# x1 in the output tensor, accumulating DMAs from GpSimd, the last bias on VectorE, and one more high half on ScalarE in each second quad

## What is computed

```
x1  = x + xattn(layernorm(x), ctx, ctx) @ wo          # 16 heads; correlation, top 4 lags, softmax, mix
h   = gelu(q16(layernorm(x1)) @ q8(W_in) + b_in)      # 256 -> 1024
out = x1 + q16(h) @ q8(W_out) + b_out                 # 1024 -> 256
```

## Time and profile before

| | |
|---|---|
| median of 3 runs | 1096.88 us (1096.68 to 1096.90) |
| the profiled execution | 1096.63 us, its span 1094.8 us |
| TensorE clock granted over the span | 0.988 |
| busy: PE, DVE, ACT, POOL | 97%, 89%, 86%, 46% of the span |
| moved by DMA | 203 GB/s over the span, 327 to 356 GB/s in most slices of part 3 |

### The profile page before, as it was taken

The page is one execution under the profiler, slowest core; times in us unless marked ns, Lnnn a source line. Parts: engine busy times, 40 slices in busy tenths (PEclk is TensorE's granted clock), DMA queues, the critical chain, the costliest instruction groups (busy, mean ns, idle before and its releaser), DMA issues.

```text
span 1094.8 us, 28979 instructions
## 1 busy us (share of the span) xinstructions
PE 1057.6 (97%) x9303; PEld 773.7 (71%) x9303; DVE 973.0 (89%) x2790; ACT 944.1 (86%) x1698; POOL 505.2 (46%) x674
## 2 busy tenths in 40 slices
PE   6999999999999999999997799999997999999998
PEld 4788778888888888887786344444443888888886
DVE  2799998888888888888888799999997999999998
ACT  4788989988888888888886588888888999999996
POOL 4888888888888888888885400000000000000000
PEclk9999999999999999999998899999998999999999
DMA  5533334433333333333330299999999899999995
GB/s 174 169 118 116 117 110 130 131 118 117 116 118 117 117 117 117 118 117 121 122 118 37 90 310 305 307 307 307 307 307 356 313 344 334 348 327 343 347 347 200
DMA packets 141426, 222.59 MB, mean 203 GB/s; under 512 B 72321, under 2 KB 92161, under 8 KB 137217
## 3 DMA queue, kind: packets, MB, share of 16 engines
q1 hardware_dynamic: 140224, 220.12, 59.4%
q10 hardware_dynamic: 1088, 1.05, 0.3%
HBM read 121.00 MB, written 83.89 MB: 187 GB/s over the span
## 4 chain that ended last, share of the span: by engine, by line
PE 61%; DVE 11%; issue 9%; ACT 2%; DMA 1%; DVEq 1%; POOL 1%; ACTq 0%; SPq 0%; POOLq 0%
PE bank L559 20%; DVE arena L1244 7%; PE bank L420 6%; PE bank L469 6%; PE bank L493 6%; PE bank L433 6%; PE bank L443 4%; PE bank L481 4%; PE bank L455 4%; PE bank L508 3%; DVE arena L1237 2%; DVE arena L1259 1%; PE bank L588 1%; ACT arena L813 1%; DMA arena<-x_scratch 1%
## 5 line engine op out<-in xcount | busy, mean ns | idle before, releaser
L588 PE MATMUL bank<-wout,arena 128*128 128x256 f16 x2048 | 236.1, 274 | 4.4 <-DVE arena L1237 3.0
L588 PEld LDWEIGHTS bank<-wout,arena 128*128 128x128 f16 x2048 | 196.4, 98 | 45.7 <-DVE arena L1244 12.2
L559 PE MATMUL bank<-arena,win 128*128 128x512 f16 x1024 | 222.5, 381 | 2.6 <-DVE arena L1195 2.6
L559 PEld LDWEIGHTS bank<-arena,win 128*128 128x128 f16 x1024 | 100.4, 98 | 124.5 <-issue 4.1
L1244 DVE SCALAR_TENSOR_TENSOR arena<-arena,wout_rel 128x512 f16<-128x512 int16 x256 | 183.1, 746 | 3.9 <-ACT arena L813 1.3
L770 ACT ACTIVATE arena<-bank,b_in_sb,z_scale 128x512 f32<-128x512 f32 x192 | 147.0, 777 | 15.2 <-PE bank L559 10.1
L608 ACT ACTIVATE arena<-bank 128x512 f32<-128x512 f32 (+1 forms) x196 | 116.0, 593 | 31.6 <-PE bank L420 25.8
L608 ACT ACTIVATE arena<-arena 128x512 f16<-128x512 f32 x192 | 114.3, 624 | 2.4 <-POOL arena L873 0.7
L806 ACT ACTIVATE arena<-arena,one 128x1536 int16<-128x1536 f32 x64 | 100.2, 1567 | 18.5 <-DVE arena L1244 15.4
L1209 DVE TENSOR_REDUCE hmax<-arena 128x1 f32<-128x1024 f32 x96 | 111.2, 1210 | 2.9 <-ACT arena L770 2.9
L813 ACT ACTIVATE arena<-arena,wout_rel 128x512 f16<-128x512 int16 x160 | 106.9, 706 | 0.0
(11 more groups left out here) (121 smaller groups left out, 2061.6 us busy)
## 6 DMA issues: line engine op xcount, KB each, us to landing
hidden_scratch<-arena SPq DMA_DIRECT2D x32, 1536.0 KB, 5.6
arena<-hidden_scratch SPq DMA_DIRECT2D x64, 768.0 KB, 7.1
arena<-in_ctx_turned SPq DMA_DIRECT2D x64, 256.0 KB, 3.0
arena<-in_x_turned SPq DMA_DIRECT2D x64, 256.0 KB, 3.5
arena<-in_x SPq DMA_DIRECT2D x64, 256.0 KB, 3.2
x_scratch<-arena SPq DMA_DIRECT2D x64, 256.0 KB, 2.0
arena<-x_scratch SPq DMA_DIRECT2D x32, 512.0 KB, 6.0
out<-arena SPq DMA_DIRECT2D x32, 512.0 KB, 4.1
```

The lines of the kernel that those rows point to most:

```text
L559: last = nc.tensor.matmul(bank[f][:, :].rearrange("p (n t) -> p n t", n=4), win16[:, f, c, :], xt[q % 3][:, s, :, c, :], start=s == 0 and ...
L588: last = nc.tensor.matmul(bank[m * 2 + k // 2][:, k % 2 * D:(k % 2 + 1) * D], gbuf[:, s, f, k * P:(k + 1) * P], wout16[:, f, :], start=f = ...
```

## The change

`x1_scratch` goes. Part 1 stores its x1 rows straight into the output tensor. In part 3 `finish` computes scale times PSUM plus b_out (read from SBUF with a broadcast over the batches) into `yq[m]`, and GpSimd adds `yq[m]` to the rows in the output with an accumulating DMA. For the last quad it is otherwise: its x1 rows are loaded back into SBUF (`last_rows`), GpSimd adds b_out to them, VectorE adds the scaled PSUM in `finish_last`, and SyncE stores them. TensorE's bias matmuls go with GpSimd's chains and the semaphores between them. `finish` now waits for the accumulating DMA of the quad before last in place of the x1 load. In quads of odd number ScalarE makes the high half of chunk 4 as well, between high 3 and `to_int` of the next quad, and VectorE doesn't.

```diff
-HIGH_ON_ACT = (1, 3, 5, 6, 7)
+HIGH_ON_ACT = ((1, 3, 5, 6, 7), (1, 3, 4, 5, 6, 7))
+HIGHS = sum(len(v) for v in HIGH_ON_ACT)
...
-        bias_f = store_x[:, 0:256]
-        bias_rest = store_x[:, 256:512]
-        bias_part = store_x[:, 512:640].bitcast(BF16)
-        bias_rows = store_x[:, 640:768].bitcast(BF16)
-        bias_cut = store_x[:, 768:896].bitcast(BF16)
-        y_rows = store_x[:, 896:960].bitcast(BF16)
-        y_part = store_x[:, 960:962].bitcast(BF16)
-        y_rest = store_x[:, 964:967]
-        y_col = store_x[:, 968:971]
+        last_rows = store_x[:, 0:1024]
...
-        act_high = lambda q, f: q * len(HIGH_ON_ACT) + (HIGH_ON_ACT.index(f) + 1)
-        dve_high = lambda q, f: q * (FC - len(HIGH_ON_ACT)) + (f + 1 - sum(g < f for g in HIGH_ON_ACT))
+        def act_high(pairs, m, f):
+
+            return pairs * HIGHS + (m * len(HIGH_ON_ACT[0]) + HIGH_ON_ACT[m].index(f) + 1)
+
+        def dve_high(pairs, m, f):
+
+            return pairs * (2 * FC - HIGHS) + (m * (FC - len(HIGH_ON_ACT[0])) + f + 1 - sum(g < f for g in HIGH_ON_ACT[m]))
...
-                sp.dma_start(x1_v[p], x1.rearrange("p b d -> p (b d)")).then_inc(s_x1_st, 16)
+                sp.dma_start(out_q[p // 2, :, p % 2 * 2 * D:(p % 2 + 1) * 2 * D], x1.rearrange("p b d -> p (b d)")).then_inc(s_x1_st, 16)
...
-            def load_x1(q, m):
-                wait(sp, s_out[m], 16 * ((q - m) // 2) if isinstance(q, int) else (q - m) * 8)
-                sp.dma_start(yq[m].rearrange("p (n k) -> p n k", n=2), rows(x1_q, q)).then_inc(s_x1_ld[m], 16)
-
-            def store(q, m):
-                wait(sp, S["c_out"], (q + 1) * 2)
-                sp.dma_start(rows(out_q, q), yq[m]).then_inc(s_out[m], 16)
...
-            sp.wait_ge(S["b_max"], QUADS * FC // 2)
-            load_x1(0, 0)
-            load_x1(1, 1)
-            def load_quad(q, m):
-                for part in range(2):
-                    load_hidden(q, m, part)
-
-            load_quad(2, 0)
-            load_quad(3, 1)
-            store(0, 0)
-            with sp.Fori(1, QUADS // 2 - 1) as i:
+            sp.dma_start(last_rows, out_q[QUADS - 1]).then_inc(s_last, 16)
+            with sp.Fori(0, QUADS // 2 - 1) as i:
                 for m in range(2):
-                    load_quad(i * 2 + (m + 2), m)
-                    load_x1(i * 2 + m, m)
-                    store(i * 2 + (m - 1), 1 - m)
-            load_x1(QUADS - 2, 0)
-            store(QUADS - 3, 1)
-            load_x1(QUADS - 1, 1)
-            store(QUADS - 2, 0)
-            store(QUADS - 1, 1)
-            for m in range(2):
-                sp.wait_ge(s_out[m], 16 * (QUADS // 2))
+                    for part in range(2):
+                        load_hidden(i * 2 + (m + 2), m, part)
+            sp.wait_ge(S["c_out"], QUADS * 2)
+            sp.dma_start(out_q[QUADS - 1], last_rows).then_inc(s_last, 16)
+            sp.wait_ge(s_last, 32)
+            sp.wait_ge(s_out[0], 16 * (QUADS // 2))
+            sp.wait_ge(s_out[1], 16 * (QUADS // 2 - 1))
...
-            def output(q, m):
+            def output(q, m, pairs):
                 wait(pe, S["c_out"], (q - 1) * 2)
                 for f in range(FC):
-                    if f in HIGH_ON_ACT:
-                        wait(pe, S["c_hi_act"], act_high(q, f))
+                    if f in HIGH_ON_ACT[m]:
+                        wait(pe, S["c_hi_act"], act_high(pairs, m, f))
                     else:
-                        wait(pe, S["c_hi_dve"], dve_high(q, f))
+                        wait(pe, S["c_hi_dve"], dve_high(pairs, m, f))
                     for s in range(2):
                         if s == 1:
                             wait(pe, S["c_lo"], q * FC + (f + 1))
                         for k in range(4):
                             last = nc.tensor.matmul(bank[m * 2 + k // 2][:, k % 2 * D:(k % 2 + 1) * D], gbuf[:, s, f, k * P:(k + 1) * P],
                                                     wout16[:, f, :], start=f == 0 and s == 0 and k % 2 == 0,
-                                                    stop=False, skip_group_check=True)
-                    if f == FC - 1:
-                        pe.wait_ge(S["bias_ready"], 1)
-                        for j in range(2):
-                            last = nc.tensor.matmul(bank[m * 2 + j][:, :].rearrange("p (b d) -> p b d", b=2), y_rows, bias_rows.unsqueeze(1).broadcast_to([P, 2, D]),
-                                                    start=False, stop=True, skip_group_check=True)
+                                                    stop=f == FC - 1 and s == 1, skip_group_check=True)
                     last.then_inc(S["c_f"], 1)
...
                 high(q, 3)
+                if 4 in HIGH_ON_ACT[m]:
+                    high(q, 4)
                 if more:
                     to_int(q + 1, 1 - m, 0)
                 high(q, 5)
...
-            pool.wait_ge(S["xm_ready"], 1)
             pool.wait_ge(S["b_out_in"], 16)
...
-            then(nc.gpsimd.tensor_copy(bias_part, b_out_sb[:, :]))
...
-            pool.wait_ge(S["y_inverse"], 1)
...
-            nc.gpsimd.tensor_scalar(y_rows, y_rows, y_col[:, 0:1], None, ALU.mult).then_inc(S["bias_ready"], 1)
+            pool.wait_ge(s_last, 16)
+            nc.gpsimd.tensor_tensor(last_rows.rearrange("p (b d) -> p b d", b=4), last_rows.rearrange("p (b d) -> p b d", b=4),
+                                    b_out_sb[:, :].unsqueeze(1).broadcast_to([P, 4, D]), ALU.add).then_inc(S["bias_added"], 1)
+
+            def add_to_out(q, m):
+                pool.wait_ge(S["c_out"], (q + 1) * 2)
+                dst = out_q[q] if isinstance(q, int) else out_q[bass.ds(q, 1)].rearrange("q l k -> (q l) k")
+                nc.gpsimd.dma_start(dst, yq[m], accum_op=ALU.add).then_inc(s_out[m], 16)
+
+            pool.wait_ge(s_x1_st, 16 * PAIRS)
+            with pool.Fori(0, QUADS // 2 - 1) as i:
+                add_to_out(i * 2, 0)
+                add_to_out(i * 2 + 1, 1)
+            add_to_out(QUADS - 2, 0)
...
-            V.reciprocal(y_inv, y_scale).then_inc(S["y_inverse"], 1)
-            def round_h(q, m, has_output=True):
+            def round_h(q, m, pairs, has_output=True):
...
                 high(0)
                 for f in range(FC):
-                    if f + 1 < FC and f + 1 not in HIGH_ON_ACT:
+                    if f + 1 < FC and f + 1 not in HIGH_ON_ACT[m]:
...
-                    wait(dve, s_x1_ld[m], 16 * ((q - m) // 2 + 1) if isinstance(q, int) else (q - m) * 8 + 16)
+                    wait(dve, s_out[m], 16 * ((q - m) // 2) if isinstance(q, int) else (q - m) * 8)
                     dve.wait_ge(S["c_f"], (q + 1) * FC)
-                V.scalar_tensor_tensor(yq[m][:, j * 512:(j + 1) * 512], bank[m * 2 + j][:, :], y_scale, yq[m][:, j * 512:(j + 1) * 512],
+                V.scalar_tensor_tensor(yq[m][:, j * 512:(j + 1) * 512].rearrange("p (b d) -> p b d", b=2), pair(m * 2 + j), y_scale,
+                                       b_out_sb[:, :].unsqueeze(1).broadcast_to([P, 2, D]), ALU.mult, ALU.add).then_inc(S["c_out"], 1)
+
+            def finish_last(j):
+                if j == 0:
+                    dve.wait_ge(S["bias_added"], 1)
+                    dve.wait_ge(S["c_f"], QUADS * FC)
+                V.scalar_tensor_tensor(last_rows[:, j * 512:(j + 1) * 512], bank[2 + j][:, :], y_scale, last_rows[:, j * 512:(j + 1) * 512],
                                        ALU.mult, ALU.add).then_inc(S["c_out"], 1)
 
-            round_h(0, 0, False)
-            round_h(1, 1)
+            dve.wait_ge(S["b_out_in"], 16)
+            round_h(0, 0, 0, False)
+            round_h(1, 1, 0)
             with dve.Fori(1, QUADS // 2) as i:
-                round_h(i * 2, 0)
-                round_h(i * 2 + 1, 1)
+                round_h(i * 2, 0, i)
+                round_h(i * 2 + 1, 1, i)
             for j in range(2):
-                finish(QUADS - 1, 1, j)
+                finish_last(j)
```

More of the change, by code:

```diff
@@ L40 @@
 C_TURN = C_HD + HD
-C_ROW = C_TURN + 1
-C_ALL = C_ROW + 6
+C_ALL = C_TURN + 1
 W_UP = 64.0
@@ L85, in constants, with xattn_ffn_kernel @@
     table[:, C_TURN] = np.where(t % NF == 0, Q_DOWN, -Q_DOWN)
-    for k in range(9):
-        table[k, C_ROW + k % 3] = 1.0
-        table[k, C_ROW + 3 + k // 3] = 1.0
     return table.astype(np.float32), inv16
-def xattn_ffn_kernel(nc, x, x_turned, ctx_turned, wq, wk, wv, wo, w_in, b_in, w_out, b_out, table, inv_table, out, x1_dram, h_dram):
+def xattn_ffn_kernel(nc, x, x_turned, ctx_turned, wq, wk, wv, wo, w_in, b_in, w_out, b_out, table, inv_table, out, h_dram):
     B, L, D = x.shape
@@ L151, in xattn_ffn_kernel @@
         one = sb("one", [P, 12], F32)
-        y_inv = one[:, 10:11]
         x_amax, wo_top, x_up, h_amax, h_up, y_scale, wo_topr, wo_part, xm_part, hm_part = [
@@ L240, in xattn_ffn_kernel @@
             xi_done xhi_done xlo_done b_mm b_gelu b_max hmax_part hmax_all h_scale c_hq c_hi_act
[L241 removed]
+            c_hi_dve c_lo c_f c_out bias_added kp_done kf_out k_done w2_done
```

(36 more changed lines are left out.)

12 lines of the change are left out of this document (removed).

## The result

The changed kernel takes 1100.3 us (median, 1097.15 to 1102.07) where the kernel before takes 1096.89 (1096.3 to 1097.81): ratio 1.003 [1.0021, 1.0038], 0.3% slower. The forecast was 1097.3 within 1093.2 to 1107.5. The range holds the result, but the likeliest case (within 0.2%, own range to 1099.5) is not what came.

The account below looks back on a forecast made before the run. The prediction took a loop over VectorE and ScalarE (r2, `to_int`, high 5, r5) to bound part 3. Its terms, +0.61 - 0.43 - 0.13 + 0.4 = +0.45 on 1096.88, gave about 1097.3 us, range 1093.2 to 1107.5.

Parts of the forecast that it names:

- the likeliest case: The forecast's main case for the whole kernel: within 0.2% of no change, 1095.3 to 1099.5 us, chance 0.47.
- The beat: Part 3, two quads: low half r2, `to_int`, high half 5, low half r5, back to r2; stays 15.3 to 15.4 us.
- Sixth high half 0: Odd quads of part 3: moving chunk 4's high half to ScalarE leaves the steady beat unchanged, 0 us.
- `finish` unchanged: Part 3: each half of `finish` still takes 0.74 us with the bias read from SBUF instead of x1.
- tail -0.43: Last quad: without the bias pair of matmuls, `finish` starts 0.43 us earlier behind TensorE.
- Start of part 2, -0.13: Where TensorE starts its long run: without GpSimd's chain beside VectorE's first roundings, 0.13 us is saved.
- Head +0.61: Quad 1, the first odd quad: the added high half on ScalarE delays low half r5 by 0.61 us, once.
- GpSimd's addition, +0.4: Quad 0 of part 3: adding the bias to the last rows hinders VectorE by 0.4 us, bounds 0 and 2.5.
- Accumulating DMAs 0: Part 3 and its end: 31 additions into the output cost 0 us, at most 4.2 us at the end.
- B: Rival: GpSimd's descriptor writing holds up VectorE's high halves in each quad, +2 to +15 us, middle 1106; chance 0.22.
- Rival A: VectorE bounds part 3, so the sixth high half gives back 0.26 us per odd quad: 1093.4 us; chance 0.18.
- Rival C: Part 3: an addition costs the DMA engines more than load and store; at twice, share 1.30, 1166 us; chance 0.08.

Follow-up runs that it names:

- e2: The changed kernel with five high halves on ScalarE in every quad, as before the change: 1099.32 us, 1.0021 of the kernel before.
- e1: The changed kernel with the last quad's rows loaded and GpSimd's addition of the bias made at the start of part 2: 1099.47 us, ratio to before 1.0027.
- e8: The changed kernel with each accumulating DMA issued as two of half the columns: 1105.79 us, 1.0081 of the kernel before.
- e5: The changed kernel without the accumulating DMA of quad 30, whose output rows stay x1: 1098.26 us, 1.0011 of the kernel before.
- e11: The kernel of e10 with 22 matmuls that nobody reads added on TensorE ahead of part 2: 1086.72 us, 0.9908 of the kernel before.
- e12: The changed kernel with only 22 matmuls that nobody reads added on TensorE ahead of part 2: 1097.94 us, 1.0005 of the kernel before.
- e6: The changed kernel with high half 5 made ahead of the next quad's first `to_int` on ScalarE: 1092.06 us, 0.9962 of the kernel before.
- e7: The kernel before with high half 5 made ahead of the next quad's first `to_int` on ScalarE: 1092.84 us, ratio 0.9967.
- e9: The kernel before with the exchange of e7 and six high halves on ScalarE in odd quads, nothing else of the change: 1089.48 us, ratio 0.9933.
- e10: The kernel of e6 with last rows loaded early, GpSimd's addition beside VectorE's reductions in part 2, quad 30 without accumulating DMA: 1089.41 us, 0.9925 of before.

## Why the prediction came out as it did

- **The beat: right.** A loop r2 - `to_int` - high 5 - r5 sets it. 15.35 stayed 15.35, the wait ahead of r5 is 1.11 - 0.66 = 0.45 (0.42 forecast), and cutting the loop gave 4.0 us in the kernel before and 8.2 in the kernel after.
- **Sixth high half 0, `finish` unchanged, tail -0.43: right** (e2; 0.74 to 0.75; -0.44). Only the last odd quad gave 0.26 more. **Start of part 2, -0.13:** -0.10.
- **Head +0.61: right in size** (e1: +0.57), but hidden under the next item in the kernel after.
- **GpSimd's addition, +0.4: the step that failed, by its size.** The bounds were 0 and 2.5, and the value was taken near L1193's 0.49. It measured 2.09, near the upper bound; the low half beside it, with two SBUF inputs, ended only 0.55 us behind the addition. Head and addition together came to 2.0 for 1.0.
- **Accumulating DMAs 0: right in the beat** (landing 9.4 of 12.4; B refuted by e8 with twice the writing). **At the end wrong by 1.3:** the sum asked only when quad 30's DMA itself lands (its landing at 1097.1 is inside the last store's), and not what it takes from the store beside it (e5).
- **Not foreseen: the clock at the start of part 2**, +1.5 in the profiled execution. e11 and e12 show what the clock is worth. Why it rose 3 us later after the change isn't settled: PE's rows ahead of it are alike in both. Nor is it settled how much of it goes with the change. From the first matmul of part 2 to 622 us the lower level cost 3.0 us of full-speed work in the kernel after and 2.8 to 3.0 in e2, e5, e6 and e8, which begin part 2 as it does, but 1.3 in the kernel before, 1.6 in e7 and 2.9 in e9, which begin it as the kernel before does. The mean granted clock of the launch is 0.9870 over 14 runs of the kernel after and 0.9881 over 58 of the kernel before, but 0.9882 over 11 runs of e2 and 0.9883 over 10 of e5; two runs of the kernel after at 0.990 took 1097.15 and 1097.86. The kernel before with the 22 matmuls, which would show how much of the 3.4 is the clock's, was not run.
- Rival A (VectorE the bound) is false for both kernels and true for e7; in e6, e9 and e10 VectorE has no wait left, with ScalarE as full. Rival C is false for the changed kernel: an addition costs a load and a store (2.07% against 2.13%), and the share rose to 0.98, not 1.30. In e8, at 2.33% a MB, its price shows in part.
- **The range.** It was open to 1107.5 for B, which didn't come, and the forecast's own case ended at 1099.5. That the range holds 1100.3 is luck: three smaller costs (addition, last landing, clock) filled the place that was kept for B.

The sum of the errors in the spans: 1.0 (head and addition) + 1.3 (last landing) + 1.5 (start of part 2, +1.36 for -0.13) - 0.3 (last odd quad) = 3.5, on top of +0.45: the 4.0 measured. The medians stand 3.4 apart.

## What to carry to other kernels

An engine that waits in a loop with another gains nothing from less work inside the waiting part: find the instruction that starts right behind its release (`to_int` behind r2) and move what the other engine wants ahead of it. One exchange of two lines was worth 4 us here, and the whole rewrite of the residual path nothing. A GpSimd addition of 2.3 to 2.4 us held up whichever VectorE instruction it met in two places, a low half with two SBUF inputs (2.09 us lost) and a cast (1.45), and lengthened no reduction; if there are reductions, place it beside them. At a kernel's end, ask what else is still moving when the last store starts.
